# All weighed sums at the end of the experts' stage, and three moved steps, in a state-space and experts layer

## The reference

```python
h = embedding(x) * sqrt(192) + positional                     # 70 ids
# mixer (state space, 24 heads of 16 channels, state of 64)
z, xBC, dt = split(rmsnorm(layernorm(h)) @ in_proj)
xBC = silu(causal_conv4(xBC) + b);  dt = softplus(dt + dt_bias)
s_t = exp(-dt_t * exp(A_log)) * s_(t-1) + dt_t * x_t (x) B_t;  y_t = s_t . C_t + D * x_t
m = (y * silu(z)) @ out_proj
v = rmsnorm(m);  h = h + m + (silu(v @ w_gate) * (v @ w_up)) @ w_down
# experts: one shared, eight routed (2 of 4 groups, 2 of 8 experts)
n = layernorm(h);  cw = weights of the two chosen experts from sigmoid(n @ gate)
h = h + shared(n) + sum_e cw[e] * ((silu(n @ w1[e]) * (n @ w3[e])) @ w2[e])
```

## Time and profile before

| | |
|---|---|
| median of 3 runs | 888.56 us (888.48 to 889.17) |
| the profiled execution | 887.77 us, its span 885.7 us |
| granted clock of PE, mean | 0.978 |
| busy, share of the span | PE 804.8 us (91%), DVE 644.8 (73%), ACT 544.2 (61%), POOL 291.6 (33%) |

### The profile page before, as it was taken

How to read it: one execution, slowest core, us unless ns; L and a number is a source line. 1 busy time by engine, 2 the same in 40 slices (tenths; PEclk the granted TensorE clock), 3 DMA queues, 4 the chain that set the end, 5 groups by cost and what they waited for, 6 DMA issues and landing times.

```text
span 885.7 us, 23129 instructions
## 1 busy us (share of the span) xinstructions
PE 804.8 (91%) x7312; PEld 661.7 (75%) x7312; DVE 644.8 (73%) x1681; ACT 544.2 (61%) x1210; POOL 291.6 (33%) x447
## 2 busy tenths in 40 slices
PE   4567999999999999999999999999999999999767
PEld 3445787878788787878778787878878787887656
DVE  5785877878777786877777787777777787776434
ACT  4636565757666575766766575776667576665312
POOL 3542232333433242343324233342324234332202
PEclk9788999999999999999999999999999999999988
DMA  7600000000000000000000000000000000000000
GB/s 253 163 1 14 2 6 19 7 17 0 22 0 5 17 5 17 3 19 0 5 17 5 17 5 17 0 19 3 5 17 5 17 3 19 0 6 10 10 1 10
DMA packets 17107, 16.77 MB, mean 19 GB/s; under 512 B 6322, under 2 KB 15416, under 8 KB 16824
## 3 DMA queue, kind: packets, MB, share of 16 engines
q1 hardware_dynamic: 17080, 16.43, 6.5%
HBM read 12.23 MB, written 4.19 MB: 19 GB/s over the span
## 4 chain that ended last, share of the span: by engine, by line
PE 57%; DVE 12%; issue 9%; POOL 8%; DMA 8%; ACT 3%; SPq 2%; POOLq 0%; DVEq 0%; ACTq 0%
PE bank L1360 26%; PE bank L1636 7%; POOL w_raw L546 7%; DVE xa L990 5%; PE bank L1528 5%; DMA tok<-tokens 5%; PE bank L1608 4%; PE bank L1517 3%; PE bank L1697 3%; PE bank L1588 3%; DMA wt_raw<-weights 2%; PE bank L1573 2%; PE bank L1597 2%; DVE w_raw L1257 2%; PE bank L1366 1%
## 5 line engine op out<-in xcount | busy, mean ns | idle before, releaser
L1047 DVE SCALAR_TENSOR_TENSOR mr<-er,gm 128x512 f32<-128x512 f32 x192 | 131.5, 707 | 34.7 <-ACT er L721 33.0
L721 ACT ACTIVATE er<-bank 128x512 f32<-128x512 f32 x192 | 109.5, 597 | 53.0 <-PE bank L1517 52.4
L1697 PE MATMUL bank<-w2t,w_raw 128*128 128x192 f32 x576 | 120.3, 332 | 10.0 <-ACT w_raw L780 7.4
L752 ACT ACTIVATE sg<-bank 128x256 f32<-128x256 f32 x96 | 36.9, 384 | 113.1 <-PE bank L1360 113.1
L1697 PEld LDWEIGHTS bank<-w2t,w_raw 128*128 128x128 f32 x576 | 90.1, 190 | 20.7 <-ACT w_raw L780 9.6
L797 ACT ACTIVATE sg<-bank 128x256 f32<-128x256 f32 x144 | 55.4, 385 | 79.1 <-PE bank L1360 77.1
L990 DVE SCALAR_TENSOR_TENSOR xa<-xr,cw_,xa 128x256 f32<-128x256 f32 x192 | 93.5, 495 | 2.6 <-ACT xa L641 0.6
L1218 DVE TENSOR_TENSOR w_raw<-sg,bank 128x256 f32<-128x256 f32 x144 | 60.1, 417 | 31.4 <-ACT sg L797 30.4
L1528 PE MATMUL bank<-mr,xd 128*32 128x128 f32 x1536 | 69.4, 286 | 12.0 <-DVE mr L1047 11.8
L1360 PE MATMUL bank<-x_h,wt_lo 128*128 128x256 f16 x288 | 79.2, 275 | 0.0
L1360 PE MATMUL bank<-x_h,w_lo 128*128 128x256 f16 x288 | 79.2, 275 | 0.0
(11 more groups left out here) (234 smaller groups left out, 2159.2 us busy)
## 6 DMA issues: line engine op xcount, KB each, us to landing
out<-w_raw SPq DMA_DIRECT2D x16, 192.0 KB, 2.0
w_raw<-weights SPq DMA_DIRECT2D x1, 1924.0 KB, 10.8
wt_raw<-weights SPq DMA_DIRECT2D x2, 962.0 KB, 16.5
pos<-position SPq DMA_DIRECT2D x16, 96.0 KB, 2.8
ri<-exponent_rows SPq DMA_DIRECT2D x4, 384.0 KB, 4.4
tok<-tokens SPq DMA_DIRECT2D x16, 70.0 KB
sums<-lj SPq DMA_DIRECT2D x16, 64.0 KB, 2.2
ri<-sums SPq DMA_DIRECT2D x64, 12.0 KB
```

What stands on the lines that cost most here:

```text
L721: act.activation(er[:, r % NER], p_d[r % 2][:].rearrange("p (h i) -> p h i", h=HG), ACT.Exp)\
L1047: ve.scalar_tensor_tensor(mr[:, r % NER], er[:, r % NER], 1.0, gm[:, r // NQ, :].unsqueeze(1).to_broadcast([128, HG, Q]), ALU.min, ALU.mult)\
L1697: ins = pe.matmul(p_ex[e][:, b * D:(b + 1) * D], hh[:, e % NHH, b * Q:(b + 1) * Q], w2t[:, e, :], start=True, stop=True)
```

## The change

ACT takes expert output 2 right behind output 1, one Silu earlier. DVE makes all four sums 5 to 8 at the end of the experts' stage, behind the hidden product of expert 8, and none in the next body. DVE makes the one-hot ahead of the swiglu instead of behind its first product. DVE makes `t` of the second sequence ahead of the split of x, and PE the state share of it ahead of the router.

```diff
@@ ACT, experts @@
-                    for out_ in {3: (0,), 5: (1,), 6: (2, 3), 7: (4,)}.get(e, ()):
+                    for out_ in {3: (0,), 5: (1, 2), 6: (3,), 7: (4,)}.get(e, ()):
@@ DVE, swiglu @@
-                    if t == 0 and p is not None:
-                        pre_onehot(p)
@@ DVE, experts @@
-                weighed_sum(c, NP)
                 hidden(c, 8)
-                weighed_sum(c, NP + 1)
+                for e in range(NP, NX):
+                    weighed_sum(c, e)
@@ DVE, body @@
                 if f is not None:
-                    masks(f, range(3))
-                if later(b):
-                    weighed_sum(b - 1, NP + 2)
-                if f is not None:
-                    masks(f, (3,))
+                    masks(f, range(4))
                     from_state(f, 0)
-                    masks(f, (4,))
-                if later(b):
-                    weighed_sum(b - 1, NP + 3, (0,))
-                if f is not None:
-                    masks(f, (5,))
-                if later(b):
-                    weighed_sum(b - 1, NP + 3, (1,))
+                    masks(f, (4, 5))
                 split_v(b)
                 mixed(b)
                 if f is not None:
                     new_state(f, 0)
                     scanned(f, 0)
+                if p is not None:
+                    pre_onehot(p)
                 swiglu(b, p, f)
...
+                if f is not None:
+                    from_state(f, 1)
                 split_x(b)
                 if f is not None:
-                    from_state(f, 1)
                     scanned(f, 1)
                     new_state(f, 1)
                 experts(b, p)
-                if f is None:
-                    weighed_sum(b, NP + 2)
-                    weighed_sum(b, NP + 3)
@@ PE, experts @@
             def experts(c, p, f):
+                if f is not None:
+                    state_share(f, 1)
...
                 ins.then_inc(router_done, 1)
-                if f is not None:
-                    state_share(f, 1)
```

More of the change, by code:

```diff
@@ L1244, in experts, with weighed_sum @@
                     masked_g(p)
-                weighed_sum(c, NP)
                 hidden(c, 8)
-                weighed_sum(c, NP + 1)
-            def weighed_sum(c, e, parts=range(NB)):
+                for e in range(NP, NX):
+                    weighed_sum(c, e)
+            def weighed_sum(c, e):
                 ve.wait_ge(ex_done, c * NX + e + 1)
@@ L1255, in weighed_sum @@
                     ve.wait_ge(out_sum, c * ND + e - NP)
-                for b in parts:
+                for b in range(NB):
                     ins = ve.scalar_tensor_tensor(acc[:, b], p_ex[e][:, b * D:(b + 1) * D], cw[:, b, e - 1:e],
                                                   acc[:, b], ALU.mult, ALU.add)
-                if NB - 1 in parts:
-                    ins.then_inc(out_sum, 1)
+                ins.then_inc(out_sum, 1)
             def split_v(b):
```

## The result

The changed kernel takes 868.59 us (median of 4 runs, 868.10 to 869.67), the kernel before beside it 888.52 us: a ratio of 0.9785, 95% interval 0.9773 to 0.9797. That is 19.9 us less; 867.0 us had been forecast, within 860 to 877. The profiled execution took 868.48 us, its span is 866.3 us.

What follows compares the result with a forecast made beforehand. PE was taken to bound the kernel through its waits: 12.0 us for tokens, 8.4 from 0.60 in each of 14 bodies and 1.2 at the end make 21.6, giving 867.0 us, range 860 to 877.

Steps and rivals of the forecast that it cites:

- What bounds: Middle body: PE busy 49.01 of 50.70 us at full clock, so only its idle and hidden stalls can be won.
- Tokens and one-hot: At the embedding: with the sums done earlier, tokens land in time and PE's waits for the one-hot go, 12.0 us.
- ACT's copy of output 2: Experts' stage: moved behind output 1, it saves PE about 0.6 us, of which some 0.3 arrive.
- t and the state share: At the router: the share fills PE's idle of 0.26 us, so gates and ups start 0.3 us earlier.
- with PE 0.3 earlier, DVE's tail becomes 0.3 earlier too: End of the convolution: DVE's wait of 0.39 us for ACT's lj follows PE, so DVE's tail moves forward too.
- The cover of 0.46 at the first tap: DVE's first convolution tap: 0.46 us of cover, just used up by the later router; 0 to 0.15 us lost.
- Hidden product 8 and ecx: End of the experts: last eight matmuls 0.41 us a body shorter, most going into a new wait for ACT's ecx.
- The term of 0.60 a body: Experts' stage up to the exponents: 0.60 us gained in each of bodies 0 to 13, 8.4 us.
- The total: Whole kernel: 21.6 us less, from 887.77 to 866.2 us profiled; median of the runs 867.0 us.
- The masks behind the sums (c): Rival, DVE between sum 8 and mask 0: late masks make the kernel slower, 893 us; chance 0.06.
- The rival (a): Experts' stage gives nothing, DVE's convolution being 0.15 late and the rest waiting for ecx: 13.2 us gained, 875.4; chance 0.15.
- the period of 49.2: Sign in the profile after: the period between stores falls from 50.7 to 49.2 us.

Runs made afterwards that it cites:

- run 3: Kernel before, with only the four sums moved to the experts' end behind hidden product 8: 876.37 us, ratio 0.9882, body 49.96 us.
- run 2: Changed kernel with the one-hot back behind the first swiglu product: 870.44 us, ratio 0.9820, body 49.82 us.
- run 1: Kernel before, with only the one-hot moved ahead of the swiglu: 886.77 us, ratio 0.9998.
- run 6: Changed kernel with ACT's copy of output 2 back behind the Silu of expert 6: 870.00 us, ratio 0.9817, body 49.56 us.
- run 5: Changed kernel with t behind the split of x and the state share behind the router again: 871.06 us, ratio 0.9813, body 49.67 us.
- run 8: Changed kernel with POOL's first addition made to wait for DVE's routing weights: 862.84 us, ratio 0.9726, body 49.30 us.
- run 10: Changed kernel with ACT's copy of the convolution's input ahead of the router's tanh: 864.68 us, ratio 0.9767, body 49.29 us.
- run 7: Changed kernel with hidden product 8 behind sum 5 again, all four sums still at the end: 869.25 us, ratio 0.9808, body 49.57 us.
- run 9: The changed kernel again, unedited, on another chip: 868.92 us, ratio 0.9802, body 49.56 us.
- run 12: Changed kernel with POOL's first addition late, ACT's copy ahead of the tanh and two third-tile taps ahead of lj: 862.38 us, ratio 0.9733.
- run 4: Kernel before, with SP issuing the next chunk's tokens and positions ahead of the store: 877.16 us, ratio 0.9883, body 49.97 us.

## Why the prediction was right, and where its steps were not

- **What bounds.** Right: PE was the bound, and what could be won were its waits. The 1.17 us a body lie within the idle of the earlier trace rows.
- **Tokens and one-hot, 12.0 us in 14 bodies, 0.86 each.** Right in mechanism, and a little too small: 0.77 from the sums' move (run 3), another 0.26 from the one-hot's place (run 2), 1.03 together. The prediction gave the one-hot's place no price of its own; it has one, which counts only when the tokens are there (run 1 against run 2). That POOL's product beside it is the reason is argued from its length alone.
- **ACT's copy of output 2.** The half that was said not to arrive did not, nor did the other: 0.00 in a middle body (run 6). In the last two bodies it gave 0.78, where 0.44 was reckoned.
- **t and the state share.** PE's 0.3 us at the router were there. The step that failed is "with PE 0.3 earlier, DVE's tail becomes 0.3 earlier too". It was argued from lj's wait of 0.39 alone, and took every DVE instruction ahead of lj at its old length. The earlier PE made POOL's addition earlier, which then stood over e_w, 0.70 us longer. Against that the small e_sum became 0.26 shorter; the net loss, 0.44, is the 0.39 that lj had waited and somewhat more. The swap brought 0.11 (run 5). With e_w short, lj does start 0.37 earlier (12.97 against 13.34, runs 8 and 10), so the step was right but for this one length. The cover of 0.46 at the first tap was called just used up, and it was: the tap starts 5.46 us behind PE's turn in both kernels, with 0.48 of wait ahead of it now; on its own it cost nothing in this order (run 10 takes that wait away, but e_w's with it, so the two are not parted there).
- **Hidden product 8 and ecx.** The direction was right, ecx takes most of it; in the middle bodies all of it (run 7). In the last two it gave 0.58, where 0.4 was reckoned.
- **The term of 0.60 a body** for these three thus measures 0.1 to 0.2: 8.4 us were reckoned and about 2 came.
- **The total, right to 1.6 us, in part by luck.** Between the spans 21.6 us were forecast and 19.4 measured. From the hm of body 0 to that of body 14, 20.4 were forecast (14 x 1.46) and 15.9 came. Behind it 1.2 were forecast and 2.0 came: 2.3 up to the hm of body 15, of which the swap explains 1.0, the copy 0.8 and the hidden product 0.6 (a little over the whole), and 0.3 lost behind it. The other 1.4 lie ahead of the first hm, where nothing was forecast; a second trace of the same kernel (run 9) starts it 0.56 us later, so that is the spread between executions and no gain of the change.
- **The masks behind the sums (c).** Reckoned: sums end at 435.5 on the old scale, no wait. Seen: the masks follow the sums directly and PE finds them ready. ACT stands idle 0.42 us ahead of its third exponential (427.22). The view puts that down to a mask, but by the kernel's code, with four buffers (NER = 4), the third needs no mask of this chunk; it follows PE's third exponent (426.72, 0.38 us long).
- **The rival (a)**, in which the experts' stage gives nothing, was nearer to the truth in that stage than the forecast, but not by its mechanism: DVE's first tap was not late.

What had been named as signs: no wait for the one-hot or the tokens, none for the copy, a new one of 0.3 at the transposition, the last eight matmuls at 1.47, the idle at the router gone, all seen. The wait for ecx is not among PE's own; it stands with the weight loads, 7.9 us in 26 cases. Not seen: the period of 49.2.

## What to carry to other kernels

When a short wait on one queue holds a transfer, look at what stands ahead of the transfer on its own queue: here issuing the tokens ahead of the store gives as much as moving four sums on DVE. When a step is moved to fill a gap, take the instructions of the other engines along that follow it in time, and see which pairs on DVE and POOL fall on one another: a gain of 0.3 us was lost by a 0.17 us instruction that met an addition on POOL. And compare bodies, not only whole runs: effects of 0.1 us a body were below the spread of the times and plain in the period. But look at the last bodies by themselves: three steps that gave 0.00 to 0.11 us in a middle body gave 0.6 to 1.0 in the last but one, and there an idle of 1.25 us was in three traces followed by a fall of the clock.

## What the hardware showed that was not expected

In these traces a DVE instruction with two inputs in SBUF stands still while a POOL instruction of about 1 us on tensors in SBUF runs, if POOL began first: e_w (128x16) lasts 0.88 us instead of 0.17 beside an addition of 0.99; a tap (128x256) about 0.65 longer in run 12; the mask (128x512) 1.02 instead of 0.69 beside POOL's product. They end 0.03, 0.29 and 0.56 us behind POOL's instruction, more with more columns, so they were held until it ended and not slowed in part. One that began first runs on at its length, as e_w in runs 5 and 10. Tensor-scalar instructions with one input in SBUF were held too: e_sum (128x2) 0.43 instead of 0.17, the one-hot 0.61 instead of 0.34, and the router's sc (128x16), which the swap brought under POOL's product, 0.32 instead of 0.17. Not held were the hidden product and lj, with one input in a bank, and a reduction. The time appears as a longer instruction, not as idle. The Trainium skill (GPSIMD Engine Reference, the table's row on SBUF interfaces) says that GpSimd shares them with VectorE and that there is contention with DVE instructions that have two SBUF inputs or run in a 2-port mode; the rows with two inputs agree. I cited that row for the sums, where it changes nothing, and not for the routing weights, where it decided. Whether the tensor-scalar instructions were held for their mode is not shown here.

In body 14 of the kernel before, and of runs 1, 3, 4 and 5, PE is idle 0.72 us at the turned x and 1.25 us at the router. In the traces of runs 1, 3 and 5 the granted clock falls from 1.00 to 0.50 in or right behind the second idle, for some 3 us; in those of the kernel before and of run 4 it stays at 1.00 with the same idle. Why, is open.
